# An attention and expert block on one core: where the first expert weights are split into two half-precision parts

## The reference

```python
logits = xf @ router_w
gate_vals, idx = jax.lax.top_k(logits, K)          # K = 2
gates = jax.nn.softmax(gate_vals, axis=-1)
for e in range(E):                                  # E = 8
    h = jax.nn.relu(xf @ w1[e] + b1[e]) @ w2[e] + b2[e]
    y = _layernorm(xf + h, gamma[e], beta[e])
    w = jnp.sum(jnp.where(idx == e, gates, 0.0), axis=-1)
    out = out + w[:, None] * y
```

## Time and profile before

| what | value |
|---|---|
| median of 3 runs | 921.68 us (920.68 to 923.33) |
| the profiled execution | 921.47 us, its span 919.7 us |
| TensorE busy | 801.1 us (87%) |
| VectorE busy | 743.3 us (81%) |
| ScalarE busy | 571.0 us (62%) |
| GpSimd busy | 504.0 us (55%) |
| mean granted TensorE clock | 0.943 of full speed |
| chain that ended last | PE 47%, DVE 28%, issue 10%, ACT 4%, DMA 3% |

### The profile page before, as it was taken

How to read it: one execution, slowest core, us unless ns; L and a number is a source line. 1 busy time by engine, 2 the same in 40 slices (tenths; PEclk the granted TensorE clock), 3 DMA queues, 4 the chain that set the end, 5 groups by cost and what they waited for, 6 DMA issues and landing times.

```text
span 919.7 us, 27974 instructions
## 1 busy us (share of the span) xinstructions
PE 801.1 (87%) x7821; PEld 684.4 (74%) x7822; DVE 743.3 (81%) x3194; ACT 571.0 (62%) x1536; POOL 504.0 (55%) x660
## 2 busy tenths in 40 slices
PE   1799999888999999999999638999999999999910
PEld 1699999875677777777777526999999999999910
DVE  2768777833789999989999752999999999999987
ACT  2633344015889999999999523666676666676610
POOL 3000000000078888888788782778877777877850
PEclk9999999998999999999999558999999999999965
DMA  8544330034011212122121226422222222222489
GB/s 181 124 80 82 61 62 1 1 115 144 23 55 54 60 57 62 54 60 60 51 63 55 63 86 206 164 80 76 79 73 76 74 74 73 80 74 76 125 299 376
DMA packets 68637, 84.19 MB, mean 92 GB/s; under 512 B 12118, under 2 KB 52745, under 8 KB 68157
## 3 DMA queue, kind: packets, MB, share of 16 engines
q1 hardware_dynamic: 52727, 53.27, 21.4%
q0 software_dynamic: 12256, 22.50, 7.9%
q10 hardware_dynamic: 3555, 7.23, 2.3%
HBM read 48.15 MB, written 35.71 MB: 91 GB/s over the span
## 4 chain that ended last, share of the span: by engine, by line
PE 47%; DVE 28%; issue 10%; ACT 4%; DMA 3%; SPq 2%; DVEq 2%; ACTq 1%; POOL 1%; POOLq 0%
PE ps L697 9%; DVE arena L1400 7%; PE ps L797 5%; DVE arena L1066 4%; PE ps L772 4%; DVE arena L1421 3%; PE ps L783 3%; PE ps L846 3%; PE ps L832 3%; PE ps L851 3%; PE ps L778 2%; DVE arena L1383 2%; PE ps L865 2%; PE ps L956 2%; PE ps L761 2%
## 5 line engine op out<-in xcount | busy, mean ns | idle before, releaser
L578 POOL DMA_INDIRECT x_slots<-arena x192 | 191.9, 1000 | 58.1 <-POOL arena L576 45.7
L607 POOL DMA_INDIRECT y_tokens<-arena x184 | 187.4, 1018 | 46.1 <-issue 45.2
L956 PE MATMUL ps<-arena 128*128 x1472 | 180.5, 276 | 0.2 <-ACT arena L1663 0.2
L956 PEld LDWEIGHTS ps<-arena 128*128 128x128 f32 x1472 | 171.6, 192 | 1.6 <-issue 0.3
L1663 ACT ACTIVATE arena<-ps,b_t 128x256 f32<-128x256 f32 x368 | 144.6, 475 | 29.1 <-PE ps L947 19.8
L697 PE MATMUL ps<-wt,arena 128*128 128x128 f32 x960 | 123.9, 289 | 12.0 <-DVE arena L1066 12.0
L697 PEld LDWEIGHTS ps<-wt,arena 128*128 128x128 f32 x960 | 118.5, 203 | 13.4 <-DVE arena L1066 13.4
L583 POOL MEMSET arena<- 128x258 f32 x1 | 0.3, 319 | 193.6 <-DVE arena L1317 193.6
L945 PE MATMUL ps<-arena 128*128 128x256 f16 x368 | 101.3, 275 | 5.1 <-DVE arena L1369 5.1
L946 PE MATMUL ps<-arena 128*128 128x256 f16 x368 | 101.2, 275 | 0.0
L947 PE MATMUL ps<-arena 128*128 128x256 f16 x368 | 101.1, 275 | 0.0
(11 more groups left out here) (216 smaller groups left out, 1785.2 us busy)
## 6 DMA issues: line engine op xcount, KB each, us to landing
arena<-x_slots SPq DMA_DIRECT2D x92, 130.0 KB
h<-h_rows SPq DMA_DIRECT2D x1, 5440.0 KB
arena<-y_tokens SPq DMA_DIRECT2D x17, 320.0 KB
out<-h ACTq DMA_DIRECT2D x17, 320.0 KB, 3.5
arena<-x_in SPq DMA_DIRECT2D x64, 84.5 KB
arena<-x_in SPq DMA_DIRECT2D x56, 78.0 KB
h_rows<-h SPq DMA_DIRECT2D x32, 128.0 KB
arena<-y_tokens SPq DMA_DIRECT2D x1, 3200.0 KB, 14.8
```

The costliest lines, as they stand in the source:

```text
L578: pool.indirect_dma_start(xs_dram, bass.IndirectOffsetOnAxis(ap=slot_i[n][0:rows, t, k:k + 1], axis=0), row[n][0:rows, k, t, :], None).the ...
L607: pool.indirect_dma_start(y_dram, bass.IndirectOffsetOnAxis(ap=y_id[n % YBUF][:, k:k + 1], axis=0), y_sl[n % YBUF][:, k, :], None, bounds_ ...
L956: ins = pe.matmul(ps[6 + m][:, 128 * k:128 * k + 128], hid[m][:, c, 128 * k:128 * k + 128], w2_sb[:, bass.ds(e, 1), c, :].rearrange("p o n ...
```

## The change

Three edits.

1. `upper_weights` is cut into three pieces (`SPLIT`), and stands at the end of ScalarE's turns 1, 2 and 3 of attention: three, three and two experts.
2. `lower_weights` is gone from VectorE. GpSimd makes the lower parts before its first scatter, each in two instructions: it multiplies the raw weights by 256 in place, waits for that (`w1_scaled`), and subtracts the upper part.
3. In the experts' turn ScalarE does `upper_half` of tile i before `relu` of tile i - 2.

```diff
+SPLIT = ((0, 1, 2), (3, 4, 5), (6, 7))
...
+            pool.wait_ge(S["w1_loaded"], 16)
+            for e in range(NEXP):
+                pool.wait_ge(S["w1_upper"], e + 1)
+                pool.tensor_scalar(w1_raw[:, e], w1_raw[:, e], W_SCALE, None, ALU.mult).then_inc(S["w1_scaled"], 1)
+                pool.wait_ge(S["w1_scaled"], e + 1)
+                pool.tensor_tensor(w1_lo[:, e], w1_raw[:, e], w1_hi[:, e], ALU.subtract).then_inc(S["w1_split"], 1)
...
-            lower_weights()
...
+            def upper_weights(p, par):
+                if p < len(SPLIT):
+                    act.wait_ge(S["w1_loaded"], 16)
+                    for e in SPLIT[p]:
+                        act.activation(w1_hi[:, e], w1_raw[:, e], ACT.Copy, scale=W_SCALE).then_inc(S["w1_upper"], 1)
...
                 at(0, decays)
+                at(1, upper_weights)
...
-            upper_weights()
...
             def tile_iteration(at):
+                at(0, upper_half)
                 at(2, relu, range(FC))
-                at(0, upper_half)
                 at(4, tile_rstd)
```

More of the change, by code:

```diff
@@ L327, in build @@
             "slots_ready rank_used lg_ready max_ready best_ready pos_ready gate_done row_copied sc0 sc1 sc2 sc3 "
-            "base_ready og_ready nb1_ready nb2_ready w1_loaded fw_loaded w1_upper w1_split "
+            "base_ready og_ready nb1_ready nb2_ready w1_loaded fw_loaded w1_upper w1_scaled w1_split "
             "cnt_ready cnt_ps tab_f_ready tab_ps pad_first pad_ready tab_ready pad_gone pad_stored xs0 "
@@ L1220, in residual @@
                 dve.tensor_tensor(hp, hp, ps[5][:, 0:PCOLS], ALU.add).then_inc(S["h1_ready"], 1)
[L1222 to L1226, removed]
             def logits_out(p, par):
```

## The result

| | kernel before | changed kernel |
|---|---|---|
| median of 22 runs | 920.82 us (914.81 to 924.33) | 924.03 us (918.58 to 935.95) |
| ratio, with 95% interval | 1 | 1.0051 (1.0033 to 1.0069) |
| profiled execution, its span | 921.47 us, 919.7 us | 932.0 us, 929.8 us |
| mean granted TensorE clock there | 0.943 | 0.936 |

By the ratio the changed kernel is slower by about half a per cent, 4.7 us; the medians are 3.2 us apart. The prediction, 920.4 us with a range up to 924.3, said "the same", and if anything 1.3 us faster: the median lies at the upper end of that range, and the move is the other way. The changed kernel's times also spread nearly twice as far as those of before (17.4 and 9.5 us). The profiled execution is the second longest of the 22.

A forecast was written before the change was run, and what follows sets the result against it. TensorE bounds attention, TensorE and VectorE nearly fill the experts, and GpSimd's last scatters end the gap between. 921.47 - 4.3 + 2.4 + 0.7 = 920.3 us, 920.5 with the median's 0.21, stated as 920.4; range 918.0 to 924.3.

The forecast's parts named there:

- The clock: Rival: a new TensorE idle in turns 2 to 4 halves its clock once, +3.4 us, 923.8 us; 6%.
- The turns without it: Attention turns 2 to 4: ScalarE's added upper parts lengthen them by 0.7, 0.6 and 1.1 us, +2.4 in all.
- the cover in turns 2 and 3: TensorE's own work hides 0.86 and 1.02 us of ScalarE's 1.59 us delay ahead of `ln1`.
- The gap: Between attention and experts: without VectorE's string of eight, the scatters end earlier, -4.3 us, bounds 0 and -4.3.
- The scatter's stall: Between attention and experts, one GpSimd scatter held by VectorE's string takes 5.23 us; without the string, 0.93 us.
- the rival of the pads: Between attention and experts: pad transfers, not VectorE's string, hold the scatter, so nothing is won back; 924.7 us; 12%.
- GpSimd: Its sixteen instructions for the lower parts, before the first scatter: 14 to 23 us for eight experts, nobody waiting.
- That it holds VectorE: Turns 2 to 4: GpSimd's instructions delay VectorE, +0.7 us, bounds 0 and 4.3; rival with all 4.3, 924.0 us, 12%.
- The experts: ScalarE's `upper_half` ahead of `relu` changes nothing: 0 us, bounds -5.9 and +1.
- the new order pays: Rival, experts: the loop turn's wait is for ScalarE, so the order gains half of 5.9 us; 917.5 us; 5%.

The follow-up runs named there:

- the run with the upper parts in turn 1: Changed kernel with ScalarE's eight upper parts all in its three idles of turn 1: 916.11 us, ratio 0.9934; again 914.41 us, ratio 0.9930.
- the run with the string back: Changed kernel with the lower parts back on VectorE as eight instructions between attention and experts, none on GpSimd: 930.79 us, ratio 1.0070.
- The second comparison of the changed kernel with before: Changed kernel unaltered, measured again beside the kernel before on one chip: 922.22 us against 921.07, ratio 0.9990.
- two parts a turn: Changed kernel with two upper parts a turn in turns 1 to 4 rather than three, three and two: 931.2 us, ratio 1.0134.

## Why the prediction was wrong, point by point

**The clock.** This is the step that failed. The prediction gave it 6%, one fall of 3.4 us, and set it aside by one row: an idle of 0.76 us at 583 us had cost nothing. One idle of that length at another place told nothing of three here: 0.80 us in turn 2 brought a fall both times it was run. The price of 3.4 us was about right for most falls, and a clock below full from 222 to 250 us stood on the list of signs; the chance and the number were wrong. The profiled execution had three falls; against the turns at full clock with the same delay (10.59, 10.95, 11.09) they cost 3.2, 3.2 and 4.8 us, the 11.2 us of difference in attention. With one fall, in turn 2, it is 290.90 - 287.95 = 3.0 us.

**The turns without it.** Forecast +2.4 us, measured +3.9 (1.5, 1.4 and 1.0, where 0.7, 0.6 and 1.1 were forecast). The mis-sized term is the cover in turns 2 and 3. I set TensorE's readiness against the end of `ln1`; but its wait is for `values_out` too, which ScalarE runs behind `ln1` and which ends half a microsecond later. The code that I had described says so. ScalarE's `values_out` of turns 2 and 3, before:

```profile
221.69 0.57 ACT L1527 ACTIVATE arena<-ps 85x512 f32<-85x512 f32 x1
...
230.76 0.58 ACT L1527 ACTIVATE arena<-ps 85x512 f32<-85x512 f32 x1
```

It ends at 222.26 and 231.34 us, so the cover is 0.38 and 0.53 rather than 0.86 and 1.02, and 1.2 and 1.1 us are left of 1.59. The other 0.3 us of each turn was not traced. In turn 4, where the row of the chain showed `values_out` as the last, the forecast was right.

**The gap.** Forecast -4.3, measured -6.0. The scatter's stall went as forecast, 5.23 us to 0.9, and the rival of the pads is dead: they are still there, and no scatter waits. Most of the other 1.7 us is the stream of scatters, which starts 5.0 us after the last `decays` rather than 6.6. It comes with sixteen more instructions on GpSimd, and even useless ones bring it. I had said of GpSimd's scatters that they just move with the rest.

**GpSimd.** The time for its work was bounded at 14 to 23 us and took 21.3: 1.50 us for the scaling, just above the upper bound, and 1.16 for the subtraction. That it holds VectorE was taken at +0.7 with a rival of 12%; measured it is under 0.2 in the run with the upper parts in turn 1, and next to nothing in turns 3 and 4 of the run with the string back.

**The experts.** Forecast 0, measured 0 in the steady tiles (260.38 against 260.39), but as a sum of two: -0.7 for the order, which the rival "the new order pays" had right in sign and far too large, and +0.7 for GpSimd's code.

**The sum.** The three mis-sized terms nearly cancel: -1.7 for the gap, +1.5 for the turns, -0.7 for VectorE. So without falls the time would have come out 0.9 us below the forecast, and in that there would have been luck. With the sizes measured, but no fall: -6.0 + 3.9 = -2.1 us, so 919.4; with one fall +0.9, 922.4; with three +9.1, which is the profiled execution (its span is 10.1 longer; the other 1.0 is the start and the end). The median lies between one fall and three. How many falls the runs without a profile had is not known, but their mean clock is: of the 22 runs of the result the four longest, 928.69 us and more, have 0.933 to 0.937, and all others 0.942 or more. The second comparison of the changed kernel with before gave no difference, the first half a per cent. That fits a number of falls that differs from run to run (three, one and two in the three profiles); the rest of each run's time moves by several microseconds in the first stage as well.

## What to carry to other kernels

A delay on an engine off the critical path is to be followed to every semaphore of the wait it feeds, the later instructions of that engine among them, not just to the one named in the change. If it opens an idle on TensorE, its price is not the idle alone but perhaps half clock for some microseconds behind it as well: 3.9 us of delay and 11.2 us of falls in the profiled execution here. So look first for a place where the engine that takes the extra work is idle already (turn 1 here), or fill the wait with products. If there is neither, spreading the work thinner is no remedy, since each wait is another chance of a fall: ratio 1.0134 with four such turns, 1.0051 and 0.9990 with three, 1.0030 with one; these do not tell one from three. An idle that cost no clock at one place is no proof for another. And work that leaves a stage takes its contention with it: a string of two-input VectorE instructions held a scatter for its whole length.

## What the runs showed of the hardware

- An idle of 0.80 to 1.32 us of TensorE, at full clock ahead of it, was followed by clock 0.50 in 12 of 19 cases in turns 2 to 4, and by nothing in the others. Ahead of tile 8, 0.22 to 1.37 us brought none in ten profiles, and 1.78 to 2.89 us one in four of seven. The Trainium skill ("TensorE: Matmul & The Clock Gate", section What's actually happening) says that what sets the clock runs free, without regard to where the kernel starts. That fits these runs, which do not test it: with the same 1.17 us in turn 3, one profile had the fall and four had not.
- Of fourteen such falls (the two after 3.92 us counted), half clock lasted some 7 us in eight, 10 in three, 14 in two (both with two parts a turn, in turn 4), and over 24 us in one, with TensorE busy all through it:

```profile
248.00:260.00 12.00, 12.00 (x52) 8.08 (x53) 4.81 (x23) 5.87 (x17) 2.27 (x2) 0.50 0.00 1
260.00:272.00 12.00, 12.00 (x88) 8.27 (x86) 6.87 (x41) 6.86 (x18) 3.89 (x6) 0.50 0.09 27
```

- Two products without use, of 0.65 us each, in each of three waits kept the clock at 1.00.
- A string of eight two-input VectorE instructions held a scatter of 0.93 us until 0.84 to 0.86 us after its end in all four profiles from undisturbed chips that have the string (5.23, 5.23, 4.68 and 4.67 us). In those without it no scatter of the gap took over 1.3 us.
- A GpSimd `tensor_scalar` of 128x512 from and to float32 took 1.50 us, and a two-input `tensor_tensor` of the same size with a half-precision output 1.16 us.
- Sixteen useless GpSimd memsets ahead of the first scatter made the gap 2.4 us shorter and the steady expert tiles 0.7 us longer.
- On one of the chips the kernel before took 1016 us instead of 921, with the clock at 0.85 in attention (260 to 560 us) and at 1.00 in the experts.
